# A grouped-routing feed-forward stage written out, with two blocks routed together a pair ahead

## The reference

```python
def gate(xf):                      # xf: 3200 x 128, after a layernorm
    scores = softmax(xf @ gw + gb)                  # 32 experts
    scores_g = scores.reshape(T, 8, 4)              # 8 groups of 4 experts
    group_scores = sum(top_k(scores_g, 2))          # per group
    keep = the 4 best groups
    indices = top_k(where(keep, scores_g, -inf), 4) # 4 best experts in them
    return scores at indices, indices
y = sum over e of cw[:, e] * ((silu(xf @ w1[e] + b1[e]) * (xf @ w3[e] + b3[e])) @ w2[e] + b2[e])
z = (silu(xf @ sw1 + sb1) * (xf @ sw3 + sb3)) @ sw2 + sb2     # shared expert
x = x + tanh(g) * (y + z)
```

## Time and profile before

| | |
|---|---|
| median of 3 runs | 6742.71 us (6737.07 to 6746.94) |
| the profiled execution | 6736.52 us, span 6734.7 us |
| span outside the stage `f1` | 6218.0 us |
| `f1`, 3868.0 to 4384.7 us of the span | 516.7 us |
| busy share of the whole span | PE 88%, PEld 60%, DVE 70%, ACT 52%, POOL 29% |
| mean granted TensorE clock, whole span | 0.938 |
| mean granted TensorE clock, `f1` | 0.78 |

### The profile page before, as it was taken

One profiled execution on the slowest core, in us unless ns is written; L12 is line 12 of the kernel. 1 busy time (PEld: TensorE's weight loads), 2 busy tenths in 40 slices (PEclk: granted clock), 3 DMA queues, 4 the chain that ended last, 5 costly groups with the idle time before them and its releaser, 6 DMA issues. The chain is left out here.

```text
span 6734.7 us, 123692 instructions
## 1 busy us (share of the span) xinstructions
PE 5947.1 (88%) x42776; PEld 4044.1 (60%) x42776; DVE 4732.6 (70%) x12652; ACT 3471.3 (52%) x5250; POOL 1972.7 (29%) x1415
## 2 busy tenths in 40 slices
PE   6999999969897999999999956768498799999996
PEld 4666666659894555555555545645388466566653
DVE  6878777867676666666666676634577777777775
ACT  3666666655553444444444433423255466666664
POOL 2222222224453222222222122334255222222220
PEclk9999999989997999999999977878699799999998
DMA  3333333220002333333333132356332333232321
GB/s 75 77 78 73 72 72 75 63 68 21 21 21 68 81 77 81 78 79 75 76 79 75 35 68 52 60 157 183 98 118 81 82 72 71 67 69 68 69 67 25
DMA packets 200964, 492.88 MB, mean 73 GB/s; under 512 B 31689, under 2 KB 135318, under 8 KB 199162
## 3 DMA queue, kind: packets, MB, share of 16 engines
q1 hardware_dynamic: 200386, 485.47, 29.5%
HBM read 270.18 MB, written 2.25 MB: 40 GB/s over the span
## 5 line engine op out<-in xcount | busy, mean ns | idle before, releaser
L850 PE MATMUL a_max<-a_stack,a_qblk 96*100 96x482 f32 (+1 forms) x4608 | 2003.5, 455 | 114.3 <-DVE a_mx L671 35.7
L550 ACT ACTIVATE a_probs<-a_scores 128x800 f32<-128x800 f32 (+1 forms) x1536 | 1281.3, 838 | 1019.0 <-PE a_scores L867 656.9
L863 PE MATMUL a_scores<-a_qblk,a_stack 128*128 128x400 f32 (+1 forms) x4608 | 1378.7, 372 | 8.1 <-POOL a_qblk L455 2.7
L665 DVE CUSTOM_DVE_ANT_0 a_dump<-a_max,a_mqf 100x482 f32<-100x482 f32 (+1 forms) x1536 | 978.5, 657 | 426.4 <-PE a_max L850 395.6
L850 PEld LDWEIGHTS a_max<-a_stack,a_qblk 96*100 96x100 f32 x4608 | 767.2, 167 | 745.1 <-issue 205.6
L671 DVE CUSTOM_DVE_ANT_0 a_dump<-a_max,a_penq 100x482 f32<-100x482 f32 (+1 forms) x1536 | 955.6, 657 | 280.9 <-PE a_max L850 261.7
L657 DVE TENSOR_REDUCE a_mx<-a_max 100x1 f32<-100x482 f32 (+1 forms) x1536 | 941.4, 654 | 257.6 <-PE a_max L850 239.8
L879 PE MATMUL a_pv<-a_probs,a_v_aug 128*32 128x200 f32 x18432 | 1051.8, 340 | 3.4 <-ACT a_probs L548 2.1
L863 PEld LDWEIGHTS a_scores<-a_qblk,a_stack 128*128 128x128 f32 (+1 forms) x4608 | 840.4, 186 | 185.6 <-issue 52.7
L1165 POOL TENSOR_TENSOR f_hb<-f_hb,f_wb 128x400 f32<-128x400 f32 x560 | 655.8, 1185 | 965.1 <-DVE f_hb L1413 490.2
L548 ACT ACTIVATE a_probs<-a_scores,a_kbias 128x800 f32<-128x800 f32 (+1 forms) x768 | 697.5, 926 | 413.6 <-PE a_scores L863 413.4
(11 more groups left out here) (302 smaller groups left out, 8471.7 us busy)
## 6 DMA issues: line engine op xcount, KB each, us to landing
a_stack<-a_khi SPq DMA_DIRECT2D x768, 180.5 KB, 3.4
a_ctxT<-in_ctxT_dram SPq DMA_DIRECT2D x128, 722.0 KB, 8.5
a_stack<-a_klo SPq DMA_DIRECT2D x384, 180.5 KB, 3.5
f_wb<-weights_by_token SPq DMA_DIRECT2D x24, 1600.0 KB, 10.7
f_wb<-weights_by_token SPq DMA_DIRECT2D x64, 400.0 KB, 6.3
a_ctxn<-in_ctxn_dram SPq DMA_DIRECT2D x32, 704.0 KB
a_mt_i<-in_mask1T_dram SPq DMA_DIRECT2D x32, 600.0 KB, 6.9
a_mq_i<-in_mask_dram SPq DMA_DIRECT2D x32, 564.1 KB
```

The source lines that it names most:

```text
L550: act.activation(out_, in_, ACT.Exp, scale=scale).then_inc(sc_free, 1)
L665: nc.vector.tensor_tensor_reduce(dump[:, k % 2, 0:n], src, mqf[:, b % 2, o:o + n], 1.0, -3.0e38, ALU.mult, ALU.max, out_).then_inc(mx_free, 1)
L850: pe.matmul(to[0:S, 0:n], qblk[0:96, b % 2, HALF * h + head, :], stack[0:96, b % 2, g, o:o + n], start=True, stop=True).then_inc(mx_full, 1)
L863: ins = pe.matmul(out_, stack[:, b % 2, 2 * h + g, kt * D:kt * D + r], qblk[:, b % 2, HALF * h + 4 * g:HALF * h + 4 * g + 4, :].rearrange( ...
```

## The change

`f1` gets a phase of its own, `grouped_ffn_phase`. The work of a tile is the same, instruction by instruction, and so are the lags. What differs:

- All 136 tiles are written out, in one numbering `g` over all blocks; two-deep buffers go by `g % 2` and not by the tile's number in its block.
- Two blocks are routed together: `QB` = 8 sequences in each routing instruction. Pair 0 is routed ahead of the tiles. Pair p is routed during the first 17 tiles of pair p - 1 (34 tiles), at tiles 8 to 16 of them; the weights of its first block are turned at tile 18, of its second at tile 23.
- The four best are found by `max`, which sorts out the 8 largest of a row in order, and `match_replace`, which overwrites the elements that equal one of 8 given values. Both work on one row at a time, so each is issued once per sequence: 8 `max` and 8 `match_replace` for the groups, and as many for the experts. `ranks` and `best` go, and with them the loads of `before`, `lower` and `rev`.
- In the opening the expert weights of parts 0, 1 and 2 are rounded before the tile loop of ScalarE and VectorE starts. On SyncE the order is: parts 0 and 1, spread of block 0, part 2, spread of block 1, parts 3 to 8. Part 3 is rounded at tile 1, part 4 at tile 3, and so on.
- The loop over `bn_stats` is written out.

```diff
+HIT = 5.0
+ABSENT = -3.0
...
+def grouped_ffn_phase(nc, name, x, ident, w, gate, scratch):
...
+    QB = 2 * BLK
+    SPLIT_LAG, DOWN_LAG, Y_LAG, TURN_LAG = 2, 3, 4, 5
+    TILES = C * NBLK
...
+        for n in range(2, NBLK):
+            at = 2 * C * (n // 2 - 1) + 4 * (n % 2)
+            xn_at[at] = n
+            turn_at[at + 1] = n
+            split_at[at + 2] = n
+            logits_at[at + 3] = n
+            low_at[at + 3] = n
+        shift_at, expo_at, score_at, keep_at, top_at, weight_at = {}, {}, {}, {}, {}, {}
+        w_turn_at, wT_at = {}, {}
+        for p in range(1, PAIRS):
+            at = 2 * C * (p - 1)
+            shift_at[at + 8] = p
+            expo_at[at + 9] = p
+            score_at[at + 10] = p
+            keep_at[at + 12] = p
+            top_at[at + 14] = p
+            weight_at[at + 16] = p
+            w_turn_at[at + 18] = 2 * p
+            wT_at[at + 19] = 2 * p
+            w_turn_at[at + 23] = 2 * p + 1
+            wT_at[at + 24] = 2 * p + 1
...
+        EARLY = 3
+        part_at = {PART * (p - EARLY) + 1: p for p in range(EARLY, len(PARTS))}
...
+            def weights_spread(n):
+                sp.wait_ge(wT_ready, n + 1)
+                sp.dma_start(scratch[n % 2][0:E, :], wT[:, n % 2, :]).then_inc(wT_out, 16)
+                sp.wait_ge(wT_out, 16 * (n + 1))
+                if n >= 2:
+                    sp.wait_ge(hw_ready, ROUTED * (n - 1))
+                for two in range(2):
+                    sp.dma_start(wb[64 * two:64 * two + 64, n % 2, :, :],
+                                 scratch[n % 2][0:E, :].rearrange("(c two) t -> two c t", two=2)[two].partition_broadcast(64)
+                                 ).then_inc(wb_in[n % 2], 16)
...
+            weights_spread(0)
+            part_load(2)
+            weights_spread(1)
+            for p in range(3, len(PARTS)):
+                part_load(p)
+            for n in range(2, NBLK):
+                weights_spread(n)
...
+            split_x(0)
+            split_x(1)
+            exponent(0)
+            round_weights(0)
+            round_weights(1)
+            weights_copy(0)
+            weights_copy(1)
+            round_weights(2)
...
+            for b in range(B):
+                mark(nc.vector.bn_stats(st[:, b, :], x[:, b, :]))
+            mark(nc.vector.memset(score[:, :, 8:12], ABSENT))
+            mark(nc.vector.memset(kept[:, :, E:E + 4], ABSENT))
+            settle()
+            rstd_steps(nc, dve, step, st, mean[:, :], rstd[:, :], tmp, var_ready, root_ready, 1e-5)
...
+            def shift_logits(p):
+                dve.wait_ge(logits_ready, 2 * p + 2)
+                logits = p_r[:, 0:QB * E].rearrange("p (b e) -> p b e", b=QB)
+                step(nc.vector.tensor_tensor(prob[:, :, :], logits, bc(brouter[:, :], 1, QB), ALU.add))
+                step(nc.vector.tensor_reduce(col[:, 0, :], prob[:, :, :], AX.X, ALU.max))
+                nc.vector.tensor_tensor(prob[:, :, :], prob[:, :, :], bc(col[:, 0, :], 2, E), ALU.subtract).then_inc(shifted_ready, 1)
+            def group_scores(p):
+                dve.wait_ge(expo_ready, p + 1)
+                step(nc.vector.tensor_reduce(col[:, 1, :], expo[:, :, :], AX.X, ALU.add))
+                step(nc.vector.reciprocal(col[:, 2, :], col[:, 1, :]))
+                step(nc.vector.tensor_tensor(prob[:, :, :], expo[:, :, :], bc(col[:, 2, :], 2, E), ALU.mult))
+                p4 = prob[:, :, :].rearrange("p b (g k) -> p b g k", k=4)
+                for far, at in ((1, 0), (2, 3), (3, 5)):
+                    mark(nc.vector.tensor_tensor(pairs[:, :, :, at:at + 4 - far], p4[:, :, :, 0:4 - far], p4[:, :, :, far:4], ALU.add))
+                settle()
+                step(nc.vector.tensor_reduce(score[:, :, 0:8], pairs[:, :, :, :], AX.X, ALU.max))
+            def keep_groups():
+                for b in range(QB):
+                    mark(nc.vector.max(top[:, b, :], score[:, b, 0:8]))
+                settle()
+                step(nc.vector.memset(top[:, :, 4:8], ABSENT))
+                for b in range(QB):
+                    mark(nc.vector.match_replace(score_hit[:, b, :], top[:, b, :], score[:, b, :], HIT))
+                settle()
+                step(nc.vector.tensor_scalar(bound[:, :, :], score_hit[:, :, 0:8], HIT, 3.0, ALU.is_equal, ALU.mult))
+                step(nc.vector.scalar_tensor_tensor(kept[:, :, 0:E].rearrange("p b (g k) -> p b g k", k=4), bc(bound[:, :, :], 3, 4), -1.0,
+                                                    prob[:, :, :].rearrange("p b (g k) -> p b g k", k=4), ALU.add, ALU.min))
+            def top_experts():
+                for b in range(QB):
+                    mark(nc.vector.max(top[:, b, :], kept[:, b, 0:E]))
+                settle()
+                step(nc.vector.memset(top[:, :, 4:8], ABSENT))
+            def weights_of(p):
+                for b in range(QB):
+                    mark(nc.vector.match_replace(kept_hit[:, b, :], top[:, b, :], kept[:, b, :], HIT))
+                settle()
+                if p > 0:
+                    dve.wait_ge(w_turned, 2 * p)
+                nc.vector.scalar_tensor_tensor(weight[:, :, :], kept_hit[:, :, 0:E], HIT, prob[:, :, :],
+                                               ALU.is_equal, ALU.mult).then_inc(weight_ready, 1)
...
+            normalise(0)
+            normalise(1)
+            low_x(0)
+            low_x(1)
+            dve.wait_ge(router_in, 32)
+            shift_logits(0)
+            group_scores(0)
+            keep_groups()
+            top_experts()
+            weights_of(0)
+            split_weights(0)
+            split_weights(1)
+            split_weights(2)
...
-        ffn("f1", "groups", 1)
+        w = {k: A[f"f1_{k}"] for k in ("wg", "wu", "wd", "router", "bg", "bu", "bd", "bshared", "brouter")}
+        grouped_ffn_phase(nc, "f1", x, ident, w, gates[0:S, 5:6], scratch)
```

310 lines of the change are left out of this document (added).

## The result

The changed kernel takes 6564.72 us (median of 4 runs, 6561.93 to 6574.34), against 6744.82 (6737.07 to 6757.22) for the kernel before in the same rounds: ratio 0.9734, 95% interval 0.9716 to 0.9752, so 180 us less. It is faster, as forecast, but by more than the 135 us of the forecast and 7 us beyond the low end of its range.

A forecast was written before the change was run, and what follows sets the result against it. Waits and the slow clock they bring were taken to bound f1, no engine being full. Opening +15 us and tiles -150 gave 135 less: 6602 profiled, 6608 as median, range 6572 to 6650.

The forecast's parts named there:

- the order of the causes: Waits in f1: GpSimd for spread weights (165.7 us), TensorE for f_hl (86.9), then the opening (40.7 without a tile, 24.3 slow).
- the two transfers in line: Opening: part 3 queues behind two spreads of 20.4 us each and stops ScalarE at tile 1 until 3947.7.
- The spread leaves the block ends: Block ends of f1: both spreads of a pair fit, the first with 3 us to spare; idle times go.
- The opening: Start of f1, before the tiles: shorter bn_stats and routing, but two spreads ahead of part 3; 15 us longer.
- The price of the sorts: Routing on VectorE: 0.18 us per max, 0.33 per match_replace; sixteen of each 8.2 us, within 14.2 for a pair.
- A pair without routing: Tiles of f1: 34 tiles at 1.645 us plus turning, router, short stalls and bias product for two blocks, 67.0 us.
- How much of a burst is felt: Tiles: TensorE feels each of five VectorE routing bursts less 0.9 us, so 9.2 of 13.7 us a pair.
- the hold and the clock: Tiles: GpSimd's hold on two-input VectorE instructions and the slow clock behind the longest burst, 2.8 us more a pair.
- the table loads: ScalarE's exponential table loads, two per pair instead of per block: counted as nothing because ScalarE idles for most of the stretch.
- bursts swallowed: Rival, tiles: VectorE catches up between bursts and the clock holds, 3 x 12 us go: 6572; 15 in 100.
- The sum: Whole f1: pair 0 79 us, pairs 1 and 2 158, pair 3 59, last tile 6; 135 us less in all.
- the Trainium skill's two rules: VectorE routing: a match replacement is two instructions; omitting a semaphore saves nothing, which would make the opening about 2 us longer.

The follow-up runs named there:

- the lead: Changed kernel with ranks, mask and four rounds of best in place of max and match_replace, still routing two blocks a pair ahead: 6630.09 us, ratio 0.9842.
- the sorts alone: Kernel before with ranks and best replaced by max and match_replace, still one block at a time in the same slots: 6652.71 us, ratio 0.9875.
- The sorts twice: Changed kernel with every max and match_replace issued a second time into a spare buffer: 6574.90 us, ratio 0.9767 to the kernel before.

## Why the prediction was wrong

The direction, the order of the causes and the two transfers in line were right; the time was 43 us too long. What failed is the size of three terms: the price of the sorts, the preparation of a pair, and how much of a burst TensorE feels. In the profiled execution the sum said 6602 and 6564 was measured. Step by step:

- **The spread leaves the block ends** (forecast: no wait of GpSimd, the idle times there go): right. GpSimd's wait of 165.7 us is gone in every version with the lead and is still there (171.5) with the sorts alone.
- **The opening** (forecast part 3 at ScalarE 79.2 us behind the first `bn_stats`): 69.0, so 10.2 less. The mechanism was right, the spreads 20.2 and 19.9 us for 20.4. Mis-sized: `bn_stats` 6.3 for 7.9, two blocks turned and multiplied 4.0 for 5.1 (3882.92 to 3886.96), routing 10.0 for 14.2, and the second spread issued 20.3 behind the first for 22.5. 1.6 + 1.1 + 4.2 + 2.2 are 9.1 of the 10.2; the rest is in terms of half a microsecond or less.
- **The price of the sorts** (0.18 and 0.33 us, lower bounds 0.10 and 0.20): 0.07 to 0.09 and 0.14 to 0.17. This is the term that failed outright: it fell out of its own bounds. Those came from rows of 0.18 to 0.21 us for small instructions, each of which waits for the one before; I took off a little for the missing waits, where most of the time goes. Sixteen of each were 8.2 us by forecast and, with the waits behind each eight, 4.3 by measurement, so 3.9 less in the opening. In the tiles the bursts of a pair add up to 9.9 us instead of 13.7 (1.4, 2.9, 2.8, 1.1 and 1.8), so 3.8 less in each pair.
- **A pair without routing** (67.0): 63.9. The 4.0 us a block that I took from `f2` for turning, router and short stalls are 2.4 here: 63.9 less 34 x 1.645 for the tiles, 2 x 0.65 and 1.8 leaves 4.9 for two blocks. That is 3.1 a pair.
- **How much of a burst is felt** ("about 0.9 is swallowed", then 2.8 for the hold and the clock): with the measured bursts this rule gives 9.9 - 4.5 + 2.8 = 8.2; measured 6.1. The 0.9 came from the earlier trace rows, where bursts stand one tile apart. The runs show no fixed amount: 0.3 us are swallowed right behind the table loads, 0.9 a tile further on or one tile behind another burst, 1.5 two tiles behind one. I had counted nothing for the table loads, since ScalarE is idle for most of a pair; the largest stop of a pair stands behind them. The rival "bursts swallowed" was the nearer one in its time, 6572, but largely by luck: of the 12 us a pair that it took away, 6.1 were still felt, and cheaper sorts and preparation made up for them. The clock was a smaller part than feared: the stop of 2.57 us brings a stretch at the lower level that costs another 1.5, and that stretch, by the reckoning under "The sorts twice", also hid the burst at tile 12.
- **The sum**: pairs 1 and 2 took 139.1 us (4018.80 to 4157.92) for 158; pair 0 78.6 (3940.22 to 4018.80) for 79, which is luck: its second block took 32.0 us like the others, cheaper than forecast, but its first, with the weight parts and a clock of 0.87, took 46.6 us, 8.6 more than block 2, where I had put 4 for the parts; the last 59.3 for 59; the last tile drains in 2 for 6. Of the 9.4 us by which pairs 1 and 2 are shorter each, 3.8 are the sorts, 3.1 the preparation and 2.1 the share of the bursts that is felt (8.2 less 6.1). In all that makes 10.2 + 18.9 + 0.4 - 0.3 + 4 = 33 us; the phase began 2.7 later than in the earlier trace rows, and the rest of the kernel took 7 less, within what it varies by. 33 - 2.7 + 7 is 37 of the 38 between 6602 and 6564.

The range failed because its low end stood on one rival alone. Cheap sorts, a cheaper preparation and swallowed bursts all point the same way, and all came true at least in part.

Of the Trainium skill's two rules, that of "Vector Engine (DVE) Microarchitecture Reference" (Built-in implementations), two instructions for a match replacement, agrees with the trace (0.08 and 0.15 to 0.18 us), but the pair costs less than one of the small instructions with a wait. The sentence of the Trainium skill's page "VectorE: DVE Perf Modes" (The DRAIN you can't avoid) that leaving out the semaphore saves nothing, the trace contradicts: eight independent `MAX8` take 0.65 us, so they start 0.07 apart at 0.15 each, while the small steps of the opening that wait for each other last 0.18 to 0.21 and start some 0.23 apart. The same section also says that a next instruction which is not held back starts earlier, and with that the trace agrees.

What stays open: how much of the stop at tile 10 the two table loads cause by themselves, since no version moved the exponential alone; why block 0 is slower when the spread of block 1 is last; and what the sorts would give in earlier slots without the pairs. A lead of three blocks and a single spread for both blocks were not tried either.

## What to carry to other kernels

When a wait hangs on a long transfer, ask when it is released: making the work ahead of it cheaper in the same slots gave nothing at the block ends, moving it a pair ahead removed the wait, and the gains of the two overlap (89 and 106 us alone, 168 together). Then look at what the earlier transfer is now queued ahead of: the order of the transfers in one queue, with the splits that it needs, was worth 22 us, once the stop was removed and not moved. Small work between the tiles is not free: 9.9 us of it cost 6.1 here in five pieces, and 11.7 with four of the pieces in one. What was swallowed grew with the distance from the last thing that made VectorE late: 0.3, 0.9 and 1.5 us. And a burst that makes no stop may lie in a stretch in which TensorE is slow, as the one at tile 12 did.

## What the runs showed of the hardware

- Independent small instructions on VectorE overlap strongly: `MAX8` of 8 elements lasts 0.15 us and starts 0.07 behind the one before, of 32 elements 0.18 and 0.09; load and replacement of a match are 0.14 to 0.17 for both; 32 `bn_stats` of 128 elements take 6.28 us, 0.20 each, where one lasts 0.29.
- One stop of TensorE of 2.57 us was followed, from 1.6 us behind it, by some ten matmuls 0.33 us apart instead of 0.18, at a clock of 0.51 over 4041.1 to 4044.5 and 0.81 over 4036 to 4045.
- Two transfers of 1600 KB each, one such spread to 128 partitions, keep the DMA engines 95% busy for 20 us (0.95 over 3900 to 3941 with two such spreads), and the part of weights queued behind one was usable 19.4 to 21.0 us after the spread's issue in every version that was profiled.
